# Both feed-forward blocks of a macaron transformer layer in two token halves, routing and combining beside the experts

## Chip, cores and metric

The kernel runs on one core of one Trainium2 chip. The metric is device time in microseconds for one execution: the median of several runs. The kernel before takes 886.95 us (3 runs, 886.47 to 887.26).

## The reference

`x` is 16 sequences of 256 tokens with 256 features, float32; a layer is a half feed-forward block, attention, and the same half feed-forward block again:

```python
x = x + 0.5 * ffn(layernorm(x), gate_w, gate_up_proj, down_proj)
x = x + attn(layernorm(x), w_qkv, w_out)        # 16 heads of 16, causal
x = x + 0.5 * ffn(layernorm(x), gate_w, gate_up_proj, down_proj)

def ffn(x, ...):                                # E = 16 experts, I = 128, TOPK = 2
    p = sigmoid(x @ gate_w.T); p = p / p.sum(-1)
    w, idx = top_k(p, 2); w = w / w.sum(-1)
    combine = sum(one_hot(idx, 16) * w)
    gate, up = split(einsum('th,ehf->etf', x, gate_up_proj))
    y = einsum('eti,eih->eth', silu(gate) * up, down_proj)
    return einsum('eth,te->th', y, combine)
```

The kernel computes only the two experts of each token that `combine` doesn't make zero.

## The kernel before

The 4096 tokens are 32 tiles of 128 (`NT`); `x` stays in SBUF (`x_sb`). Five engines run in-order programs joined by semaphores: PE (matmul), ACT, DVE, POOL and SP, which issues plain DMAs. The order is written by hand: each engine's program is the order of the calls.

A feed-forward block has four stages. In words, with the functions of each engine:

1. Moments and logits. DVE takes moments of `x_sb` (`moments`, 8 token tiles at a time), POOL their inverse root (`inverse_root`, `rstd`), DVE writes the normalised rows (`normalised`, four tiles a round, two buffers `rows`). SP stores them in HBM (`store_normed`, tensor `normed`); a buffer of `rows` is written again only when its store has landed. PE turns the rows (`route_transposes`, L708, four PSUM banks), ACT copies them out (`route_copies`, L846, `xnT`), PE makes logits (L717), ACT copies (L852), PE turns them back (L733), ACT takes the sigmoid (L862).
2. The choice. DVE finds the two best experts of all tokens (L978 to L988), their weights, counts per expert (L997 on, after two PE matmuls), and a slot for each token and choice (L1008 to L1023). Tokens are sorted by expert into tiles of 128 slots. An expert's last tile may be part empty, so there are at most `NE_T` = 4096 x 2 / 128 + 16 = 80 tiles. The expert of each tile is in `eid`.
3. One hots. For each pair of token tile and choice, DVE (L1032, L1033) and ACT (`second_parts`, L880 and L885) make one-hot matrices, and PE adds their product (L750) into a bank, which yields for each slot the token that fills it: `source` (L1043). There are 64 pairs, eight at a time.
4. Tiles. For each of the 80 tiles POOL gathers 128 rows of `normed` by an indirect DMA (`fetch`, L632, a ring of four buffers `xe`), PE turns them (`transpose_in`, L767), ACT copies (`evac_in`, L868, `xeT`), PE multiplies by the expert's weights, which it picks by a register (`gate_up_mm`, L774), ACT takes silu (L872), DVE the product (`gated`, L1049, `hid`), PE turns it (`transpose_hid`, L780), DVE copies (`evac_hid`, L1053, `hidT`), PE multiplies (`down_mm`, L785), DVE copies the result (`evac_out`, L1058, `ye`), SP stores it (`store`, L576, `grouped_out`). PE's order in step j is `transpose_in(j+1)`, `gate_up_mm(j)`, `transpose_hid(j-1)`, `down_mm(j-2)`. PSUM banks, `xeT`, `hid` and `hidT` are double.

Each token's two result rows must come back from `grouped_out`, by indirect DMA on POOL from `slot`, and are added with their weights on DVE. For the first block that is done in attention (`attn_pool` FETCH, L294; `attn_vector` MIX, L497 and L502), two token tiles a sequence. For the last block it follows the tiles: 64 gathers (L649, a ring of eight), two DVE operations a tile (L1081, L1084), and SP stores `out`.

Ahead of attention ACT rearranges the query and key weights (L439) and DVE fills the three `kT` buffers with ones (L488); two of these buffers and the block's work buffers share one memory (`shared`), the third and the raw weights share `spare`. Attention is ordered by tables (`PE_TURN` and others), in which a step is (offset of the sequence, kind, number); they stay as they are.

## Time and profile before

| what | us |
|---|---|
| median of 3 runs | 886.95 |
| the profiled execution, time | 886.32 |
| the profiled execution, span | 884.6 |
| PE busy in the span | 662.1 (75%) |
| DVE busy | 574.8 (65%) |
| ACT busy | 366.6 (41%) |
| POOL busy | 395.4 (45%) |
| first block, first tile turned | 88.06 |
| attention, first rows turned | 242.24 |
| last block, first rows turned | 592.03 |
| last block, first tile turned | 660.34 |
| last block, first gather of results | 798.02 |

Busy shares are means over stages that differ: PE is busy nearly without a gap in the tiles and in attention and idle in the rest. So a stage is to be read by itself, with what each engine waits for in it. PEld is the load of weights into PE, which overlaps the matmuls before; its start shows best when PE takes up a piece of work. The granted clock is the share of 2.4 GHz that PE had: 1.0 is 2.4, 0.5 is 1.2 GHz.

### The profile page before, as it was taken

To read this page: it belongs to the slowest core of one execution; us is meant where nothing else is said; L and a number is where in the kernel's file an instruction comes from. 1 tells how busy PE (TensorE), PEld (TensorE's weight loads), DVE (VectorE), ACT (ScalarE), POOL (GpSimd) and SP (SyncE) were. 2 spreads that over 40 slices of the span, in tenths; PEclk is the share of its full clock that TensorE was granted. 3 is DMA by queue.
4 is the path that set the end of the run, shared out by engine and by line. 5 is a ranking of instruction groups with operands and counts; after the bars stand their busy time and mean duration, and the time that the engine had idled before them with its cause. 6 is when DMAs were issued, how large, how long until landed. Compare 5 with 4: busy or idle time off the path is not lost.

```text
span 884.6 us, 17856 instructions
## 1 busy us (share of the span) xinstructions
PE 662.1 (75%) x5016; PEld 507.6 (57%) x5017; DVE 574.8 (65%) x1599; ACT 366.6 (41%) x941; POOL 395.4 (45%) x467
## 2 busy tenths in 40 slices
PE   2614999999078999999999999866159999990000
PEld 2402888887056777777777777544038888870000
DVE  6597455555758888878888877646964555553333
ACT  2417334444025555555656655454263333430000
POOL 4101655553453554444555422240026555536775
PEclk9955999999678999999999999988559999995555
DMA  7680455557263444444444433014004555574554
GB/s 238 219 258 10 142 162 162 160 160 137 65 185 106 132 128 120 121 116 129 114 109 121 113 107 97 4 48 144 0 24 142 162 162 161 161 130 130 153 152 142
DMA packets 94136, 113.36 MB, mean 128 GB/s; under 512 B 11633, under 2 KB 84609, under 8 KB 94081
## 3 DMA queue, kind: packets, MB, share of 16 engines
q1 hardware_dynamic: 80224, 74.87, 27.5%
q0 software_dynamic: 13824, 37.77, 17.5%
q8 instruction: 31, 0.51, 0.2%
q14 instruction: 25, 0.20, 0.1%
q10 hardware_dynamic: 32, 0.02, 0.0%
HBM read 49.30 MB, written 33.55 MB: 94 GB/s over the span
## 4 chain that ended last, share of the span: by engine, by line
PE 64%; DVE 12%; DMA 8%; issue 5%; POOL 5%; ACT 4%; SPq 1%; DVEq 0%; ACTq 0%; POOLq 0%
PE bank L774 16%; PE bank L785 8%; PE bank L352 6%; PE bank L411 5%; PE bank L372 5%; PE bank L397 5%; PE bank L767 4%; POOL shared L649 4%; DMA shared<-grouped_out,slot 3%; PE bank L359 3%; PE bank L375 3%; PE bank L431 3%; PE bank L780 2%; DMA normed<-shared 2%; ACT shared L885 1%
## 5 line engine op out<-in xcount | busy, mean ns | idle before, releaser
L632 POOL DMA_INDIRECT shared<-normed,source x160 | 152.3, 952 | 213.4 <-DVE source L1043 111.2
L774 PE MATMUL bank<-wgu_sb,xeT 128*128 x640 | 167.8, 386 | 0.0
L306 POOL TENSOR_SCALAR_AFFINE_SELECT pr<-pr 128x512 f32<-128x512 f32 x128 | 81.0, 655 | 154.8 <-ACT pr L476 154.6
L534 DVE TENSOR_REDUCE mx<-bank 128x2 f32<-128x512 f32 (+1 forms) x192 | 127.0, 685 | 23.6 <-PE bank L375 20.4
L1053 DVE COPY hidT<-bank 128x128 f32<-128x128 f32 x160 | 46.6, 291 | 116.8 <-PE bank L780 115.9
L774 PEld LDWEIGHTS bank<-wgu_sb,xeT 128*128 128x128 f32 x640 | 111.5, 194 | 8.8
L476 ACT ACTIVATE pr<-bank 128x512 f32<-128x512 f32 x192 | 102.9, 609 | 30.6 <-PE bank L397 18.1
L785 PE MATMUL bank<-wd_sb,hidT 128*128 x320 | 95.6, 382 | 0.0
L868 ACT COPY xeT<-bank 128x256 f32<-128x256 f32 x160 | 59.5, 372 | 84.6 <-PE bank L767 84.3
L294 POOL DMA_INDIRECT gathered_rows<-grouped_out,slot x64 | 69.0, 1078 | 27.8 <-DMA grouped_out<-shared 13.4
L872 ACT ACTIVATE silu<-bank 128x128 f32<-128x128 f32 x160 | 44.4, 278 | 83.2 <-PE bank L774 83.2
L649 POOL DMA_INDIRECT shared<-grouped_out,slot x64 | 61.3, 958 | 32.4 <-issue 16.1
L767 PE MATMUL bank<-ident,shared 128*128 128x128 f32 x320 | 63.1, 280 | 9.4 <-DMA shared<-normed,source 9.3
L1058 DVE COPY shared<-bank 128x256 f32<-128x256 f32 x160 | 67.9, 424 | 3.5 <-PE bank L785 0.7
L352 PE MATMUL bank<-anT,wqk 128*128 128x256 f32 x256 | 63.4, 394 | 1.9 <-ACT anT L447 1.9
L375 PE MATMUL bank<-future,ident_b 128*128 128x256 bf16 (+1 forms) x192 | 61.3, 319 | 0.0
L767 PEld LDWEIGHTS bank<-ident,shared 128*128 128x128 f32 x320 | 45.1, 144 | 27.5 <-issue 9.3
L411 PE MATMUL bank<-pr,v_sb 128*32 128x256 f32 (+1 forms) x1024 | 54.9, 332 | 3.3 <-POOL pr L306 3.3
L372 PE MATMUL bank<-shared 112*128 112x256 bf16 (+1 forms) x352 | 52.7, 255 | 4.1 <-DMA shared<-parts 3.3
L785 PEld LDWEIGHTS bank<-wd_sb,hidT 128*128 128x128 f32 x320 | 48.3, 191 | 12.4 <-issue 0.4
L1049 DVE TENSOR_TENSOR hid<-bank,silu 128x128 f32<-128x128 f32 x160 | 45.3, 283 | 15.5 <-ACT silu L872 15.5
L352 PEld LDWEIGHTS bank<-anT,wqk 128*128 128x128 f32 x256 | 48.4, 198 | 8.7 <-ACT anT L447 2.8
(148 smaller groups left out, 1118.2 us busy)
## 6 DMA issues: line engine op xcount, KB each, us to landing
grouped_out<-shared SPq DMA_DIRECT2D x160, 128.0 KB, 1.7
shared<-parts SPq DMA_DIRECT2D x154, 128.0 KB
spare<-parts SPq DMA_DIRECT2D x70, 128.0 KB
normed<-shared SPq DMA_DIRECT2D x16, 512.0 KB, 3.1
x_sb<-in_L_attn_x_dram SPq DMA_DIRECT2D x4, 1024.0 KB, 9.7
wgu_sb<-_L_ffn_gate_up_proj_dram SPq DMA_DIRECT2D x8, 512.0 KB, 8.6
out_dram<-x_sb SPq DMA_DIRECT2D x16, 256.0 KB, 2.6
shared<-normed,source POOLq DMA_INDIRECT x160, 2.8
```

The lines of the kernel that those rows point to most:

```text
L306: nc.gpsimd.affine_select(out=m, in_=m, compare_op=ALU.is_ge, fill=0.0, base=0, pattern=[[0, 4], [1, P]], channel_multiplier=-1).then_inc( ...
L352: last = nc.tensor.matmul(dst[:, e * S:(e + 1) * S], wqk[:, c, x, e, :], anT[:, c, :], start=(c == 0), stop=(c == HC - 1))
L372: nc.tensor.matmul(dst[:, i * w:(i + 1) * w], q[0:ROWS, h0 + i, u * P:(u + 1) * P], k[0:ROWS, h0 + i, 0:w], start=(i == 0), stop=False, sk ...
L375: nc.tensor.matmul(diag, ident_b[:, :], future[:, 0:nh, :], start=False, stop=True, skip_group_check=True).then_inc(at["score_done"], 1)
L411: last = nc.tensor.matmul(bankC[j * VW:(j + 1) * VW, cols + kt * P:cols + S], v_sb[b % 2][:, kt, 4 * n + j, :], rhs, start=(kt == 0), stop ...
L476: nc.scalar.activation(dst.rearrange("p h n -> p (h n)"), bank[n % 3][:, :], ACT.Exp).then_inc(at["exp_ready"], 1)
L534: nc.vector.tensor_reduce(mx[:, u, h0:h0 + nh], bank[3 + n % 2][:, :].rearrange("p (h k) -> p h k", h=nh), AX.X, ALU.max).then_inc(at["max ...
L632: nc.gpsimd.indirect_dma_start(xe[:, r, :], None, normed, bass.IndirectOffsetOnAxis(source[:, j:j + 1], 0)).then_inc(s["xe_loaded"][r], 16)
L649: nc.gpsimd.indirect_dma_start(late[:, t % LATE, j, :], None, grouped_out, bass.IndirectOffsetOnAxis(slot[:, t, j:j + 1], 0)).then_inc(s[" ...
L767: last = nc.tensor.transpose(bank[u][:, c * P:(c + 1) * P], xe[:, r, c * P:(c + 1) * P], ident[:, :])
L774: last = nc.tensor.matmul(bank[2 + u][:, 0:2 * I], xeT[:, u, c, :], wgu_sb[:, e, c, :], start=(c == 0), stop=(c == HC - 1))
L785: nc.tensor.matmul(bank[6 + u][:, 0:H], hidT[:, u, :], wd_sb[:, e, :], start=True, stop=True).then_inc(s["down_done"], 1)
```

## The change

Each feed-forward block runs in two halves of 16 token tiles (`HT`), A and B, each with its own `normed`, `grouped`, slots and at most `NH` = 47 tiles; `ES` = 94 tiles a block run in one sequence. The routing of a half is cut into parts (moments, rows, top, counts, one hots and so on), and each engine has a table of (step, part, number). `route` runs a table's parts one after the other: half A, ahead of the tiles. `route_beside` runs those of half B inside the tile loop, after the tile work of the given step. In the last block POOL gathers the results of 13 token tiles of half A in the steps of `GATHER_AT` (53, 56, ... 89), and DVE combines 12 of them in the steps of `COMBINE_AT` (57, 60, ... 90).

Banks are fewer per use: the routing's transposes have bank 5 alone, the tiles' transposes bank 0, `transpose_hid` bank 3 and `down_mm` bank 4. The output copy `evac_out` goes from DVE to ACT. SP loads half A of `x`, then all expert weights, then stores half A's rows, then loads half B of `x` and attention's weights. The fills with ones are written as 32x2048 float32 words: one at the program's start, two at step 49 of the first block. `wqk_in` lies in `gathered_rows`, and the first gather of attention waits for its conversion. Loops with registers are unrolled, the helper `after` is written out, and attention's parts are otherwise the same.

```diff
-def macaron_block(nc, x_in, w_qkv, w_out, gate_w, gate_up, down, out, stages=("ffn", "attn", "ffn")):
...
     EW = 32
-    NE_T = B * S * TOPK // P + E
     RING = 4
-    NK = NE_T // RING
-    LOADS = 4
+    HT = NT // 2
+    NH = (HT * P * TOPK + E * (P - 1)) // P
+    ES = 2 * NH
+    GATHER_AT = range(NH + 6, NH + 45, 3)
+    COMBINE_AT = range(NH + 10, NH + 46, 3)
     LATE = 8
     PLACES = 8
     EPS = 1e-5
...
+    grouped = [nc.dram_tensor(f"grouped{h}", [NH * P, H], F32).ap() for h in range(2)]
 
     ctx = ExitStack()
     with ctx:
...
-        wqk_in = spare[:, 0:HC * 2 * H].rearrange("p (c f) -> p c f", c=HC)
+        wqk_in = gathered_rows[:, 0:2, :, :].rearrange("p r k h -> p (r k h)").rearrange("p (c f) -> p c f", c=HC)
+        ye, xe = (spare[:, i * RING * H:(i + 1) * RING * H].rearrange("p (r h) -> p r h", r=RING) for i in range(2))
...
-            for r in range(RING):
-                dve.wait_ge(ffn[0]["ye_stored"][r], 16 * NK)
-            dve.wait_ge(at["wqk_ready"], 2 * HC)
-            for i in range(BUFS):
-                last = nc.vector.memset(kT[i][ROWS // 32 * 32:P, :, :], 1.0)
-            last.then_inc(at["ones_set"], 1)
...
+        DVE_ROUTE = [(0, STATS, 0), (1, MOMENTS, 0), (2, STATS, 1), (3, NORMALISE, 0), (4, MOMENTS, 1), (5, STATS, 2),
+                     (6, NORMALISE, 1), (7, MOMENTS, 2), (8, STATS, 3), (9, NORMALISE, 2), (10, MOMENTS, 3),
+                     (12, NORMALISE, 3), (19, TOP, 0), (21, TOP, 1), (23, PICKS, 0), (24, WEIGHTS, 0), (26, COUNTS, 0),
...
+        ACT_ROUTE = [(4, TURNED, 0), (7, TURNED, 1), (8, LOGITS, 0), (10, TURNED, 2), (11, LOGITS, 1), (13, TURNED, 3),
+                     (14, LOGITS, 2), (15, LOGITS, 3), (17, SIGMOID, 0), (32, ONEHOT, 0), (35, ONEHOT, 1), (38, ONEHOT, 2),
...
+        PE_ROUTE = [(4, TURNED, 0), (7, TURNED, 1), (7, LOGITS, 0), (10, TURNED, 2), (10, LOGITS, 1), (10, LOGITS_T, 0),
...
+        POOL_ROUTE = [(5, MOMENTS, 0), (8, MOMENTS, 1), (11, MOMENTS, 2), (14, MOMENTS, 3)]
+        SP_ROUTE = [(1, STORE, 0), (4, STORE, 1), (7, STORE, 2), (10, STORE, 3)]
...
+        def route(table, part, g):
+
+            for _, kind, n in table:
+                part(kind, n, g)
+
+        def route_beside(table, part, j, g):
+
+            for at_step, kind, n in table:
+                if at_step == j:
+                    part(kind, n, g)
+
+        def tile_at(f, j):
+
+            return f * ES + j, j // NH, j % NH, 2 * f + j // NH
...
+            def part(kind, n, g):
+                if kind == STORE:
+                    R = g * ROUNDS + n
+                    sp.wait_ge(s["xn_ready"], RING * (R + 1))
+                    sp.dma_start(normed[g % 2].rearrange("(n p) h -> p n h", p=P)[:, n * RING:(n + 1) * RING, :],
+                                 rows[:, R % 2, :, :]).then_inc(s["xn_stored"][R % 2], 16)
+
+            route(SP_ROUTE, part, 2 * f)
...
+                for c in range(HT // RING, NT // RING):
+                    load_x(sp, c)
+                sp.dma_start(wqk_in, w_qkv.rearrange("(c p) f -> p c f", p=P)[:, :, 0:2 * H]).then_inc(wqk_loaded, 16)
+                sp.dma_start(wv[:, :, :], w_qkv.rearrange("(c p) f -> p c f", p=P)[:, :, 2 * H:3 * H]).then_inc(wv_loaded, 16)
+                sp.dma_start(wout_sb[:, :, :], w_out.rearrange("(c p) f -> p c f", p=P)).then_inc(wout_loaded, 16)
+            for j in range(ES):
+                G, p, jj, g = tile_at(f, j)
+                route_beside(SP_ROUTE, part, j, 2 * f + 1)
+                sp.wait_ge(s["ye_ready"], G + 1)
+                sp.dma_start(grouped[p][jj * P:(jj + 1) * P, :], ye[:, G % RING, :]).then_inc(s["ye_stored"][G % RING], 16)
...
+            for c in range(HT // RING):
+                load_x(sp, c)
+            for e in range(0, E, 4):
+                for c in range(HC):
+                    sp.dma_start(wgu_sb[:, e:e + 4, c, :],
+                                 gate_up[e:e + 4, c * P:(c + 1) * P, :].rearrange("e p f -> p e f")).then_inc(wgu_loaded, 16)
+                sp.dma_start(wd_sb[:, e:e + 4, :], down[e:e + 4].rearrange("e i h -> i e h")).then_inc(wd_loaded, 16)
...
+            def gather(t):
+                if t == 0:
+                    stored_through(pool, ES + NH)
+                if t == HT:
+                    stored_through(pool, 2 * ES)
+                if t - LATE + 1 > 0:
                     pool.wait_ge(s["x_done"], t - LATE + 1)
                 for j in range(TOPK):
-                    nc.gpsimd.indirect_dma_start(late[:, t % LATE, j, :], None, grouped_out,
+                    nc.gpsimd.indirect_dma_start(late[:, t % LATE, j, :], None, grouped[t // HT],
                                                  bass.IndirectOffsetOnAxis(slot[:, t, j:j + 1], 0)).then_inc(s["gathered"][t % LATE], 16)
+
+            route(POOL_ROUTE, part, 2 * f)
+            for j in range(ES):
+                G, p, jj, g = tile_at(f, j)
+                if jj == 0:
+                    pool.wait_ge(s["source_ready"], g + 1)
+                    for i in range(2):
+                        pool.wait_ge(s["xn_stored"][i], 16 * (ROUNDS // 2) * (g + 1))
+                if G - RING + 1 > 0:
+                    pool.wait_ge(s["xe_transposed"], G - RING + 1)
+                nc.gpsimd.indirect_dma_start(xe[:, G % RING, :], None, normed[p],
+                                             bass.IndirectOffsetOnAxis(source[:, p, jj:jj + 1], 0)).then_inc(s["xe_loaded"][G % RING], 16)
+                route_beside(POOL_ROUTE, part, j, 2 * f + 1)
+                if f == 1 and j in GATHER_AT:
+                    gather(GATHER_AT.index(j))
+            if f == 1:
+                for t in range(len(GATHER_AT), NT):
+                    gather(t)
...
+            def part(kind, n, g):
+                R = g * ROUNDS + n
+                if kind == TURNED:
+                    for r in range(RING):
+                        pe.wait_ge(s["xn_ready"], R * RING + r + 1)
+                        if R * RING + r > 0:
+                            pe.wait_ge(s["xnT_ready"], R * RING + r)
+                        for c in range(HC):
+                            last = nc.tensor.transpose(bank[5][:, c * P:(c + 1) * P], rows[:, R % 2, r, c * P:(c + 1) * P], ident[:, :])
+                        last.then_inc(s["xn_transposed"], 1)
...
+                elif kind == ONEHOT:
+                    for r in range(PLACES):
+                        i = n * PLACES + r
+                        pe.wait_ge(s["onehot_ready"], g * HT * TOPK + i + 1)
+                        if r % TOPK:
+                            pe.wait_ge(s["second_ready"], g * HT + i // TOPK + 1)
+                        nc.tensor.matmul(bank[7][:, 0:NH], is_part[:, r, :], is_tile[:, r, 0:NH], start=(i == 0),
+                                         stop=(i == HT * TOPK - 1), skip_group_check=True).then_inc(s["source_done"], 1)
...
+            def transpose_in(j):
+                G, p, jj, g = tile_at(f, j)
+                pe.wait_ge(s["xe_loaded"][G % RING], 16 * (G // RING + 1))
+                if G > 0:
+                    pe.wait_ge(s["xeT_ready"], G)
...
+                    last = nc.tensor.transpose(bank[0][:, c * P:(c + 1) * P], xe[:, G % RING, c * P:(c + 1) * P], ident[:, :])
+                last.then_inc(s["xe_transposed"], 1)
...
+            transpose_in(0)
+            read_expert(0)
+            for j in range(ES + 2):
+                if j + 1 < ES:
+                    transpose_in(j + 1)
+                if j < ES:
+                    gate_up_mm(j)
+                if j + 1 < ES:
+                    read_expert(j + 1)
+                if 0 <= j - 1 < ES:
+                    transpose_hid(j - 1)
+                if 0 <= j - 2 < ES:
+                    down_mm(j - 2)
+                route_beside(PE_ROUTE, part, j, 2 * f + 1)
...
+            def part(kind, n, g):
+                R = g * ROUNDS + n
+                if kind == TURNED:
+                    for r in range(RING):
+                        act.wait_ge(s["xn_transposed"], R * RING + r + 1)
+                        if R - 1 > 0:
+                            act.wait_ge(s["logitsT_done"], R - 1)
+                        nc.scalar.copy(xnT[:, R % 2, r, :, :].rearrange("p c n -> p (c n)"), bank[5][:, 0:H]).then_inc(s["xnT_ready"], 1)
...
+                elif kind == SIGMOID:
+                    act.wait_ge(s["logits_done"], ROUNDS * (g + 1))
+                    if g > 0:
+                        act.wait_ge(s["picks_ready"], g)
+                    nc.scalar.activation(prob[:, :, :], bank[7][:, :].rearrange("p (t w) -> p t w", w=EW)[:, :, 0:E], ACT.Sigmoid)\
+                        .then_inc(s["prob_ready"], 1)
...
+                    act.sem_inc(act_turn, 1)
+                    for q in range(m):
+                        nc.scalar.activation(distance[:, q, :], lane_h[:, :], ACT.Abs, bias=minus_part[:, n * m + q:n * m + q + 1])\
+                            .then_inc(s["distance_ready"], 1)
+                    for q in range(m):
+                        act.wait_ge(s["distance_ready"], i + q + 1)
+                        if i * TOPK + q * TOPK + 2 - PLACES > 0:
+                            act.wait_ge(s["source_done"], i * TOPK + q * TOPK + 2 - PLACES)
+                        nc.scalar.activation(is_part[:, q * TOPK + 1, :], distance[:, q, :], ACT.Relu, scale=-1.0, bias=one_e[:, 0:1])\
+                            .then_inc(s["second_ready"], 1)
...
+            def evac_out(j):
+                G, p, jj, g = tile_at(f, j)
+                act.wait_ge(s["down_done"], G + 1)
+                if 16 * (G // RING) > 0:
+                    act.wait_ge(s["ye_stored"][G % RING], 16 * (G // RING))
+                nc.scalar.copy(ye[:, G % RING, :], bank[4][:, 0:H]).then_inc(s["ye_ready"], 1)
...
+            evac_in(0)
+            for j in range(ES + 2):
+                if j + 1 < ES:
+                    evac_in(j + 1)
+                if j < ES:
+                    silu_gate(j)
+                if 0 <= j - 2 < ES:
+                    evac_out(j - 2)
+                route_beside(ACT_ROUTE, part, j, 2 * f + 1)
...
+            route(DVE_ROUTE, part, 2 * f)
+            for j in range(ES + 1):
+                if 0 <= j - 1 < ES:
+                    evac_hid(j - 1)
+                if j < ES:
+                    gated(j)
+                route_beside(DVE_ROUTE, part, j, 2 * f + 1)
+                if f == 0 and j == NH + 2:
+                    for i in range(2):
+                        dve.wait_ge(s["xn_stored"][i], 16 * ROUNDS)
+                        nc.vector.memset(kT_words[i], TWO_ONES).then_inc(at["ones_set"], 1)
+                if f == 1 and j in COMBINE_AT:
+                    combine(COMBINE_AT.index(j))
+            if f == 1:
+                for t in range(len(COMBINE_AT), NT):
+                    combine(t)
...
```

Three places in the engines' programs, word for word (line numbers are those of each kernel).

SP at the start of the program; `x_sb` is the input, `wgu_sb` and `wd_sb` the expert weights, `normed` the stored rows. Before:

```order
L600 DMA x_sb<-in_L_attn_x_dram 128x8x256 x4
L578 UNCONDITIONAL_BRANCH
L578 ISA
L571 ISA
L571 DMA normed<-shared 128x4x256
```

And in the change:

```order
L613 DMA x_sb<-in_L_attn_x_dram 128x4x256 x4
L621 DMA wgu_sb<-in_L_ffn_gate_up_proj_dram 128x4x256 x2
L623 DMA wd_sb<-in_L_ffn_down_proj_dram 128x4x256
L621 DMA wgu_sb<-in_L_ffn_gate_up_proj_dram 128x4x256 x2
L623 DMA wd_sb<-in_L_ffn_down_proj_dram 128x4x256
L621 DMA wgu_sb<-in_L_ffn_gate_up_proj_dram 128x4x256 x2
L623 DMA wd_sb<-in_L_ffn_down_proj_dram 128x4x256
L621 DMA wgu_sb<-in_L_ffn_gate_up_proj_dram 128x4x256 x2
L623 DMA wd_sb<-in_L_ffn_down_proj_dram 128x4x256
L595 DMA normed<-shared 128x4x256 x4
```

The twelve weight loads, which stood behind all stores of rows, now stand ahead of the first.

ACT beside the tiles of half A, steps 16 to 18 (`shared<-bank` of L861 is the sigmoid of half B, `spare<-bank` the output copy). Before there was only the pair of copy and silu for each tile:

```order
L868 COPY xeT<-bank 128x256
L872 ACTIVATE silu<-bank 128x128
L867 REGISTER_ALU
L868 COPY xeT<-bank 128x256
L872 ACTIVATE silu<-bank 128x128
```

In the change:

```order
L884 COPY xeT<-bank 128x256
L889 ACTIVATE silu<-bank 128x128
L896 COPY spare<-bank 128x256
L861 ACT_TABLE_LOAD
L861 ACTIVATE shared<-bank 128x256
L884 COPY xeT<-bank 128x256
L889 ACT_TABLE_LOAD
L889 ACTIVATE silu<-bank 128x128
L896 COPY spare<-bank 128x256
```

The output copy has joined, and a sigmoid with two loads of the function table stands between two tiles.

POOL in the last block; `spare<-normed` or `shared<-normed` is the fetch of a tile, `<-grouped` a gather of results. Before:

```order
L621 TENSOR_TENSOR rstd<-var,minus_half 128x8 x4
L632 DMA shared<-normed,source 128x256 x80
L649 DMA shared<-grouped_out,slot 128x256 x64
```

In the change, from the fetches behind the last root to the end (the pair of rows that repeats is shown twice):

```order
L667 DMA spare<-normed,source 128x256 x39
L655 DMA shared<-grouped,slot 128x256 x2
L667 DMA spare<-normed,source 128x256 x3
L655 DMA shared<-grouped,slot 128x256 x2
L667 DMA spare<-normed,source 128x256 x3
```

```order
L655 DMA shared<-grouped,slot 128x256 x2
L667 DMA spare<-normed,source 128x256 x4
L655 DMA shared<-grouped,slot 128x256 x38
```

26 of the 64 gathers have moved in between the fetches, two for every three fetches.

## Rows read from the trace of the kernel before

**Rows 1.** Stretches: each engine's busy us (x instructions), then clock, DMA share, GB/s

```profile
634.00:657.00 23.00, 11.81 (x64) 6.25 (x64) 20.66 (x101) 20.84 (x65) 0.00 (x0) 0.50 0.01 1
661.00:795.00 134.00, 133.31 (x718) 111.29 (x718) 70.53 (x240) 51.98 (x160) 73.57 (x77) 0.98 0.56 153
```

**Rows 2.** Timeline of one tile: start, us, engine line operation xcount [idle before]

```profile
151.62 0.36 PEld L767 LDWEIGHTS bank<-ident,shared 128*128 128x128 f32 x2
...
152.26 0.37 ACT L868 COPY xeT<-bank 128x256 f32<-128x256 f32 x1 [0.48 <-PE bank L767]
...
152.71 0.14 PEld L780 LDWEIGHTS bank<-ident,hid 128*128 128x128 f32 x1
...
153.23 0.29 DVE L1053 COPY hidT<-bank 128x128 f32<-128x128 f32 x1 [0.77 <-PE bank L780]
153.25 0.36 PEld L767 LDWEIGHTS bank<-ident,shared 128*128 128x128 f32 x2
153.44 0.28 DVE L1049 TENSOR_TENSOR hid<-bank,silu 128x128 f32<-128x128 f32 x1
```

**Rows 3.** Timeline, last block: the last output matmuls, the first and last gather

```profile
793.61 1.21 PE L785 MATMUL bank<-wd_sb,hidT 128*128 x4
...
798.02 0.95 POOL L649 DMA_INDIRECT shared<-grouped_out,slot  x1 [13.20 <-DMA grouped_out<-shared]
...
877.58 0.96 POOL L649 DMA_INDIRECT shared<-grouped_out,slot  x1 [0.30 <-issue]
```

**Rows 4.** Timeline, last block: start of the choice, first fetch, first transpose

```profile
613.83 0.69 DVE L978 TENSOR_REDUCE top<-shared 128x32 f32<-128x512 f32 x1 [3.72 <-ACT shared L862]
...
657.31 1.02 POOL L632 DMA_INDIRECT shared<-normed,source  x1 [55.59 <-DVE source L1043]
...
660.34 0.66 PE L767 MATMUL bank<-ident,shared 128*128 128x128 f32 x2 [4.13 <-DMA shared<-normed,source]
```

**Rows 5.** Timeline, first block: the first tile is turned

```profile
88.06 0.66 PE L767 MATMUL bank<-ident,shared 128*128 128x128 f32 x2 [4.30 <-DMA shared<-normed,source]
```

**Rows 6.** Timeline between the first block's tiles and attention

```profile
220.22 2.24 ACT L439 ACTIVATE wqk<-spare 128x256 f32<-128x256 f32 x4
...
220.99 1.20 PE L785 MATMUL bank<-wd_sb,hidT 128*128 x4
...
229.98 3.47 DVE L488 MEMSET shared<- 32x4096 bf16 x1 [0.80 <-issue]
...
237.75 0.88 DVE L497 SCALAR_TENSOR_TENSOR mix<-gathered_rows,weight,x_sb 128x256 f32<-128x256 f32 x2
...
242.24 1.08 PE L342 MATMUL bank<-ident,an 128*128 128x128 f32 x4 [20.04 <-DVE an L519]
```

**Rows 7.** Timeline, last block's routing: rows turned and copied at two clocks

```profile
592.03 3.28 PEld L708 LDWEIGHTS bank<-ident,shared 128*128 128x128 f32 x16 [4.50 <-DVE shared L934]
...
592.76 3.36 ACT L846 COPY shared<-bank 128x256 f32<-128x256 f32 x8 [4.95 <-PE bank L708]
...
601.36 1.17 PEld L708 LDWEIGHTS bank<-ident,shared 128*128 128x128 f32 x8 [0.66 <-DVE shared L934]
...
601.84 1.34 ACT L846 COPY shared<-bank 128x256 f32<-128x256 f32 x4 [0.88 <-PE bank L708]
```

**Rows 8.** Tile `x_sb`: ns min/median/max, first and last start; then landing times

```profile
L600 SPq DMA_DIRECT2D x_sb<-in_L_attn_x_dram x4: 447/1338/2832, 0.8 to 4.1; - x4
...
DMA to landing us min/median/max: 6.0/9.7/11.6
```

**Rows 9.** Timeline, last block's routing: a root, logits, and rows that wait

```profile
595.24 1.76 POOL L621 TENSOR_TENSOR rstd<-var,minus_half 128x8 f32<-128x8 f32 x1 [1.93 <-DVE var L931]
...
598.28 0.65 PE L717 MATMUL bank<-shared,gwT 128*32 128x128 f32 x16
...
605.68 1.38 DVE L934 TENSOR_SCALAR shared<-x_sb,mean,rstd 128x256 f32<-128x256 f32 x4 [1.94 <-DMA normed<-shared]
```

**Rows 10.** Timeline, first block: ACT loads its function table

```profile
83.36 1.28 ACT L893 ACT_TABLE_LOAD   x1
```

847 lines of the change are left out of this document (358 added, 489 removed).

## The prediction, made before the changed kernel was run

> **What bounds the kernel now.** I read the stages first [rows 1]: in the last block's tile stage PE is busy for 133 of 134 us at a clock of 0.98, while ACT, DVE and POOL have time left. One tile then shows the order in which they need each other [rows 2]: its first weight load is at 151.62, the next tile's at 153.25, so a tile costs **1.63 us** and PE sets it. The 80 tiles of the last block take from 660.34 to 794.82 = 134.5 us [rows 3, 4]. Ahead of that stands the routing: moments and logits to 613.8, a chain of DVE operations on 128x512 to 634, one hots up to the first indirect fetch at 657.31, which takes 3.0 us to the transpose [rows 4]. PE idles or waits in most of it. Behind it stand 64 gathers that POOL issues one per 1.263 us ((877.58 - 798.02)/63) until the span ends at 884.6 [rows 3]. The first block has its first tile at 88.06 [rows 5] and a hole of 20.05 us of PE, 222.19 to 242.24, before attention [rows 6]. So the places to win are real: routing, hole and tail. But what hides them must be laid beside a PE with nothing to spare.
>
> **More tiles.** A half needs (16x128x2 + 16x127)/128 = 47 tiles, so a block does 94 for 80. 14 x 1.63 = 22.8, both blocks **+45.6**. Nothing hides it: PE sets the pace. Certain to some 2 us.
>
> **The routing of half A** comes alone before the tiles. In the last block: four rounds of moments, root and rows, but PE turns each of 16 token tiles through one bank and waits for ACT's copy of the one before. One such turn is the start of the load to the start of the copy (0.73 at 592.03, low clock; 0.48 at 601.36, high clock), the copy 0.37 [rows 2], and I allow 0.05 for the way back: 1.15 or 0.90 [rows 7]. 16 x 1.15 = 18.4 and 3.9 for logits and their tail, 22.3; all 32 tiles take 21.8 now (592.03 to 613.83). The DVE chain has half the elements: 0.69 becomes 0.42 (between 0.28 for 128x128 and 0.69 for 128x512), 20.3 becomes 13.5. Of the 23.1 of one hots ACT's 64 operations are 20.9 (20.84 busy [rows 1]), so half A needs 10.4 + 2.2; the fetch 3.0 as now. 51.4, less 0.6 of shorter first moments, against 68.3 from 592.03 to 660.34: **-17.5**. At the high clock throughout 4 more; bounds -17 and -22.
> In the first block SP issues 12 weight loads (6.3 MB) right behind 2.1 MB of x. The four x loads now, 4.2 MB issued in 6 us, land up to 11.6 us after their issue [rows 8], the last near 15.7: some 280 GB/s, and they queue. So the 8.4 MB are in near 30 us; the first rows stored come behind them, and rows of round 2 wait for that store, as they do now at 605.68 [rows 9]. Round 2 at 31, turns of rounds 2 and 3 to 41, tail 3.5, chain 13.5, one hots 12.6, fetch 3.0: first tile near 73.6, **-14.5**. If stores are not held up, 63: -25.
> The Trainium skill (DMA: Bandwidth & Descriptors, "Queues, rings and completion order") says that each DMA engine consumes one ring's descriptors in order, though a later one may finish its write earlier; the landing times agree. By it the stores wait; without it this term is -25 and the sum 946.
>
> **Routing of half B beside A's tiles.** Engines are in order, so a lump delays the next tile's work once it is longer than the gap. Gaps from one tile [rows 2]: DVE has `hid` done 0.47 into a tile's period and must have served the next `hidT` and `hid` by 1.08 of the one after: a lump of up to 1.7 is free. ACT now also copies the outputs: 0.37 behind a down_mm that is 0.6 long [rows 3] and follows the load at 1.08, so from 0.4 to 0.8 of the next period. Its copy of `xeT`, then done at 1.2, must be there at 1.63: a lump of L costs L - 0.45. PE has no gap: all it does or waits for counts. Per half, in order:
> - the root on POOL (between 0.72 and 1.76, about 1.05 [rows 9]) waits for DVE's moments ahead of fetch 6: 0.7.
> - 4 times TURNED: PE sits in it while PE and ACT alternate, three turns of 0.90, the last load 0.2 and 0.35 for ACT's output copy: 3.25, x 4 = 13.0. NORMALISE (1.38 for four [rows 9]) is inside DVE's gap.
> - logits: 4 x 0.6 [rows 9], four turns 0.1 each, and 1.1 once where PE waits for ACT's copy of round 2: 3.8.
> - SIGMOID: two table loads of 1.28 [rows 10] with a sigmoid and a copy of 0.37 between them: 2.1.
> - DVE lumps: TOP 2.7 and 2.25, COUNTS 2.7, SLOT 2.7, over 1.7 by 1.0 + 0.6 + 1.0 + 1.0, and 0.5 of PE: 4.1.
> - ONEHOT 4 times: ACT's eight at 0.326 (20.84 busy for 64 [rows 1]) = 2.6, costs 2.1; PE then waits for DVE's twelve (2.3) to 3.0 of a period of 1.62: 1.4. 3.5 x 4 = 14.1.
> - source numbers come at step 45, the fetch takes 3.3 more, tile 47 is wanted at 46: 2.5.
> Sum 40.3, both blocks **+80.6**. Lower bound: PE's own instructions alone, 32 turns x 0.11, logits 2.4, turns, counts and ids 0.9, 32 placings x 0.1 = 9.9, so 20 in both. Upper bound: the same with PE at 1.2 GHz for a while, below. I take the sum, since each lump is in the queue of an engine that a tile needs.
> Of table loads the Trainium skill (ScalarE: Activation LUTs, "What ACT_TABLE_LOAD costs") says 1.28 us for the load and 1.38 more for a drain. In this trace the row shows 1.28 and starts right behind the operation before it. By the page the sum would be 5.5 higher.
>
> **Hole before attention.** The three memsets leave it: two go into half B's tiles. 32x2048 float32 has no row: by elements it is half of the 3.47 of 32x4096 bf16, by bytes the same, and each may bring its 0.8 gap [rows 6]. Two by elements, one gap hidden, are 4.0, less the free 1.7: **+2.3**; bounds 0 and +6.8. But `wqk_in` now lies in `gathered_rows`, so the gathers wait for ACT's four wqk conversions behind its last output copy: 0.45 + 2.24 after PE's end. First gather at +2.8, the fourth landed at +9.6 (three more at 1.26 and 3.0); from MIX to PE it is 4.5 now (237.75 to 242.24), and the root stands behind eight gathers, 0.4 more: +14.5 against 20.05, **-5.5**. Late next is the gather, not DVE. Between 0 and -16.
>
> **Tail.** In half B of the last block 13 token tiles are gathered between fetches, and 12 combined. For three tiles POOL has 3 fetches and 2 gathers, 6.3 us, for PE's 4.9: POOL becomes the pace. Count from tile 50's transpose: fetch 53 at 0.6, then 66 issues x 1.26, the last fetch goes out at 83.8. Its tile needs 3.0, three periods of 4.9 and a store and start of 3.2 (794.82 to 798.02), so half B's rows can be gathered from 94.9 (six gathers of half A fit in between); 32 x 1.26 = 40.3, and 7.0 from the last issue's start to the end less its 1.26: 141.0. Without hiding it would be 73.5 (PE's tiles) + 89.8 (794.82 to 884.6) = 163.3. **-22.3**; all 26 hidden free would be -33.
>
> **Sum.** 884.6 + 45.6 + 80.6 + 2.3 - 14.5 - 17.5 - 5.5 - 22.3 = 953.3. The profiled execution took 886.32 for its span of 884.6 (+1.7), and the median of the runs is 0.6 above it: **956 us**, 7.7% slower. Attention's order and PE's instructions there are the same and I count 0.
>
> **Rivals.**
> A. Half of the lumps is absorbed (ACT and DVE catch up more than I allow, the four fetched tiles buffer): beside-cost 25 a half, 925. For it: DVE is busy for 53% and ACT for 39% of the stage [rows 1]. Against: averages; the chain of one tile has only the gaps above.
> B. The clock falls. In the one hots PE is half busy and the granted clock is 0.50, in the tiles 0.98 [rows 1]. Beside TURNED and ONEHOT PE waits again and again. At 1.2 GHz a PE-paced tile is twice 1.63; for a dozen tiles a half +19, 994.
> C. The cover holds: beside-cost 9.9 a half, 892.5 + 2.3 = 895, still 0.9% slower.
> D. Faster. As C, and stores are not queued behind the weights (-10) and A's turns run at the high clock (-4): 881. It decides from a beside-cost of 13 us a half downward, with both early starts.
> E. Only the stores are free: 946.
>
> **How the numbers follow.** The sum as worked out, 940 to 972: 0.49. E 0.07, A 0.19, B 0.12, C 0.06, D 0.06, rest 0.01. The range 900 to 990 leaves out C and D and the upper half of B. Under 0.2% (1.8 us) a measurement can't tell from no change. Faster 0.06, same 0.01, slower 0.93.
>
> **What would show it.** A tile period of 1.63 in half B of the first block and 94 transposes a block; the first tile near 73 and, in the last block, 54 after its first moments; A's 47 tiles taking near 117 us where B's take 77; PE waiting for ACT's `xnT` copy between turns; a wait for `normed` of 10 us or more on DVE near 17 to 31; the first gather behind L439; POOL with no idle from fetch 53 on. The forecast is wrong if A's 47 tiles take under 95 us or over 140, if the clock in them is under 0.9, or if POOL waits for PE in the last half.

## The result, and the profile after

The changed kernel takes **959.1 us** (median of 4 runs, 954.2 to 963.0) beside 887.1 for the kernel before on the same chip: ratio 1.081, interval 1.075 to 1.086. The prediction was 956. The profiled execution took 954.18 for a span of 952.4 at a mean clock of 0.93; 953.3 was forecast for the span. It is the fastest of the four: the median is 3.1 above the forecast. What follows compares spans.

The stages of the changed kernel, in the columns of [rows 1] (a stretch, busy us of PE, PEld, DVE, ACT and POOL with instructions, granted clock, DMA share, GB/s). In order: routing of half A, A's tiles, B's tiles, the hole, attention, and in the last block half A's routing, A's tiles, B's tiles with the combine, the tail.

```profile
0.00:71.00 71.00, 21.36 (x137) 10.59 (x137) 36.58 (x145) 19.75 (x55) 12.32 (x34) 1.00 0.60 195
71.00:185.00 114.00, 94.43 (x547) 71.66 (x548) 54.95 (x231) 61.36 (x192) 49.50 (x52) 0.99 0.42 124
185.00:270.00 85.00, 81.67 (x435) 67.61 (x435) 27.40 (x99) 44.70 (x144) 42.14 (x45) 0.98 0.55 146
270.00:284.00 14.00, 0.17 (x1) 0.00 (x0) 3.16 (x11) 2.46 (x5) 8.72 (x10) 0.60 0.31 92
284.00:632.00 348.00, 326.61 (x3040) 241.95 (x3040) 269.05 (x620) 190.36 (x402) 154.04 (x200) 0.99 0.39 108
632.00:683.00 51.00, 20.29 (x135) 10.09 (x135) 28.75 (x119) 18.47 (x54) 5.13 (x6) 0.56 0.13 44
683.00:800.00 117.00, 97.12 (x549) 73.58 (x550) 50.47 (x215) 61.37 (x193) 50.53 (x52) 0.94 0.40 121
800.00:902.00 102.00, 83.62 (x433) 64.65 (x431) 35.87 (x125) 46.33 (x144) 73.10 (x77) 1.00 0.60 163
902.00:952.00 50.00, 0.38 (x2) 0.00 (x0) 17.60 (x37) 0.37 (x1) 30.66 (x32) 0.52 0.56 173
```

The second and the seventh row are the beside-stages: PE is busy for 83% there and not for 99 as in [rows 1], and PE is the engine that sets the pace of a tile. B's tiles in the first block (third row) are again nearly all PE. In B's tiles of the last block POOL has 77 operations and PE is at 82%.

| stretch | before | after | forecast | measured |
|---|---|---|---|---|
| start to the first tile | 88.06 | 71.02 | -14.5 | -17.0 |
| first block's tiles | 134.1 | 199.2 | +65.4 | +65.0 |
| hole before attention | 20.05 | 14.4 | -5.5 | -5.7 |
| attention | 349.8 | 348.1 | 0 | -1.7 |
| last block, first turn to first tile | 68.3 | 50.7 | -17.5 | -17.6 |
| last block, first tile to the end | 224.3 | 269.1 | +40.8 | +44.8 |
| sum | 884.6 | 952.4 | +68.7 | +67.8 |

**Start.** Timeline of the changed kernel (start, us, engine, line and operation, in brackets the idle time before it and who ended it): DVE's rows of round 2, the first fetch, the first turn of a tile.

```profile
29.18 1.38 DVE L958 TENSOR_SCALAR shared<-x_sb,mv,rstd 128x256 f32<-128x256 f32 x4 [14.40 <-DMA normed<-shared]
...
68.02 1.16 POOL L667 DMA_INDIRECT spare<-normed,source  x1 [35.88 <-DVE source L1027]
...
71.02 0.29 PEld L772 LDWEIGHTS bank<-ident,spare 128*128 128x128 f32 x2 [3.67 <-issue]
```

DVE stood 14.4 us for the store of round 0's rows, as in [rows 9], where it was 1.94. The first tile is at 71.02, where [rows 5] has 88.06.

**A's tiles.** The copies of `xeT`, one a tile, give the period: in B's tiles of the first block it is 1.62 or 1.63 in 42 of 46 cases. In A's tiles it is not. One lump of four turns, then one lump of one hots, both in the first block:

```profile
80.81 0.36 PEld L732 LDWEIGHTS bank<-ident,shared 128*128 128x128 f32 x2
...
81.49 0.38 ACT L851 COPY shared<-bank 128x256 f32<-128x256 f32 x1
...
81.98 0.20 PEld L732 LDWEIGHTS bank<-ident,shared 128*128 128x128 f32 x2 [0.82 <-issue]
...
83.90 0.20 PEld L732 LDWEIGHTS bank<-ident,shared 128*128 128x128 f32 x2 [0.76 <-issue]
...
84.38 0.37 ACT L851 COPY shared<-bank 128x256 f32<-128x256 f32 x1 [0.59 <-PE bank L732]
...
84.65 0.38 ACT L884 COPY xeT<-bank 128x256 f32<-128x256 f32 x1
```

```profile
158.49 1.28 ACT L872 ACTIVATE shared<-lane_h,minus_part 128x128 f16<-128x128 f16 x4
...
159.66 1.26 ACT L878 ACTIVATE shared<-shared,one_e 128x128 f16<-128x128 f16 x4
160.83 0.35 ACT L884 COPY xeT<-bank 128x256 f32<-128x256 f32 x1
...
161.30 0.20 PEld L772 LDWEIGHTS bank<-ident,spare 128*128 128x128 f32 x2 [1.90 <-issue]
```

In the first, PE's turns go out at 80.81 and then one per 0.96, each after ACT's copy; ACT copies the tile's `xeT` only at 84.65, 4.79 after the one before. In the second, ACT's eight operations sit ahead of `xeT` and PE waits 1.90. The sigmoid between two tiles, with its two table loads:

```profile
119.65 1.28 ACT L861 ACT_TABLE_LOAD   x1
120.94 0.38 ACT L861 ACTIVATE shared<-bank 128x256 f32<-128x256 f32 x1
...
121.61 1.28 ACT L889 ACT_TABLE_LOAD   x1
122.90 0.28 ACT L889 ACTIVATE silu<-bank 128x128 f32<-128x128 f32 x1
```

All the excess over 1.63, by stretches of tiles:

| beside A's tiles | forecast | first block | last block |
|---|---|---|---|
| root, turns, logits (tiles 5 to 18) | 17.5 | 16.8 | 18.4 |
| sigmoid (18 to 22) | 2.1 | 2.1 | 2.1 |
| choice on DVE (22 to 33) | 4.1 | 2.7 | 2.7 |
| one hots (33 to 46) | 14.1 | 13.8 | 13.9 |
| fetch for tile 47 | 2.5 | 1.8 | 1.7 |
| the first five tiles | 0 | 0.0 | 0.7 |
| sum | 40.3 | 37.1 | 39.5 |

**The two fills** beside half B (the fills of [rows 6], as float32 words; the second starts at 194.34), and the transposes of `hid` that waited:

```profile
192.20 1.76 DVE L1059 MEMSET shared<- 32x2048 f32 x1 [0.48 <-issue]
...
196.68 0.14 PEld L798 LDWEIGHTS bank<-ident,hid 128*128 128x128 f32 x1 [2.75 <-DVE hid L1038]
...
199.06 0.23 PEld L798 LDWEIGHTS bank<-ident,hid 128*128 128x128 f32 x1
```

A fill takes 1.76. Both together hold PE for 2.75, and the tile behind runs with weight loads of 0.23 where 0.14 is usual, a low clock, which costs 1.6 more: 4.4 in all for 2.3 forecast. The 1.6 doesn't come every time: in the profile of experiment 7 the same two fills cost 2.8 and the tile behind them takes 1.63.

**The hole.** The last output matmul, ACT's conversion, the first gather, the second mix, PE's first transposes of attention; in [rows 6] the gather did not wait for ACT, and the mix waited for DVE's fills:

```profile
269.48 0.69 PE L806 MATMUL bank<-wd_sb,hidT 128*128 x2 [0.66 <-ACT spare L896]
...
270.48 2.19 ACT L427 ACTIVATE wqk<-gathered_rows 128x256 f32<-128x256 f32 x4
272.94 0.94 POOL L271 DMA_INDIRECT gathered_rows<-grouped,slot  x1 [13.57 <-ACT wqk L427]
...
279.51 0.48 DVE L483 SCALAR_TENSOR_TENSOR mix<-gathered_rows,weight,x_sb 128x256 f32<-128x256 f32 x1 [2.10 <-DMA gathered_rows<-grouped,slot]
...
284.53 1.09 PE L322 MATMUL bank<-ident,an 128*128 128x128 f32 x4 [14.36 <-DVE an L506]
```

**The last half.** POOL, last block: the first gather of half A beside half B's tiles, the last fetch, the last gather that needs no result of B, the first that does. Then the waits of that stage (us in all, times, longest).

```profile
808.07 0.96 POOL L655 DMA_INDIRECT shared<-grouped,slot  x1 [2.87 <-DMA grouped<-spare]
...
890.31 0.96 POOL L667 DMA_INDIRECT spare<-normed,source  x1 [0.30 <-issue]
...
897.88 0.96 POOL L655 DMA_INDIRECT shared<-grouped,slot  x1 [0.30 <-issue]
905.34 0.95 POOL L655 DMA_INDIRECT shared<-grouped,slot  x1 [6.50 <-DMA grouped<-spare]
```

```profile
PEld bank L772 <- DMA spare<-normed,source: 24.5, 18, 3.1
...
POOL shared L655 <- DMA grouped<-spare: 2.9, 1, 2.9
POOL spare L667 <- PE bank L772: 1.5, 5, 0.3
```

Between 808 and 898 POOL is never idle for more than 0.31, in line with the forecast. The 1.5 us for PE are five gaps of 0.3, as long as the 0.30 that stand before its other issues, so PE never held it up. PE waits 24.5 for fetched rows. The first gather holds POOL for 2.87, since A's last results are still being stored, and the last fetch leaves 15.0 us before B's results are in.

### The profile page after: what moved, and what is told of

The parts are those of the page before. It is cut to its first block, busy times and chain, and to the rows that moved or that the text cites. A ratio compares the mean times of both kernels' runs of the same rounds, so it can differ in the third digit from the quotient of the medians.

```text
span 952.4 us, 17170 instructions
## 1 busy us (share of the span) xinstructions
PE 725.6 (76%) x5274; PEld 540.1 (57%) x5274; DVE 523.8 (55%) x1599; ACT 445.2 (47%) x1189; POOL 426.2 (45%) x503
## 3 DMA queue, kind: packets, MB, share of 16 engines
q0 software_dynamic: 15168, 41.44, 17.6%
## 4 chain that ended last, share of the span: by engine, by line
PE 59%; DVE 11%; POOL 9%; DMA 6%; ACT 6%; issue 6%; SPq 2%; POOLq 0%; ACTq 0%; DVEq 0%
PE bank L789 11%; PE bank L806 6%; PE bank L399 5%; PE bank L333 5%; PE bank L355 5%; PE bank L383 5%; POOL shared L655 4%; PE bank L772 3%; POOL spare L667 3%; DMA spare<-normed,source 3%; PE bank L358 3%; PE bank L340 3%; PE bank L419 3%; PE bank L732 2%; PE bank L798 2%
## 5 line engine op out<-in xcount | busy, mean ns | idle before, releaser
L667 POOL DMA_INDIRECT spare<-normed,source x188 | 180.7, 961 | 237.8 <-PE bank L772 140.4
L789 PE MATMUL bank<-wgu_sb,xeT 128*128 x752 | 200.8, 391 | 0.0
L806 PE MATMUL bank<-wd_sb,hidT 128*128 x376 | 116.3, 391 | 1.7 <-ACT spare L896 1.3
L772 PE MATMUL bank<-ident,spare 128*128 128x128 f32 x376 | 76.4, 286 | 43.1 <-DMA spare<-normed,source 28.6
L896 ACT COPY spare<-bank 128x256 f32<-128x256 f32 x188 | 69.9, 372 | 61.3 <-PE bank L806 61.3
L772 PEld LDWEIGHTS bank<-ident,spare 128*128 128x128 f32 x376 | 49.8, 145 | 70.7 <-DMA spare<-normed,source 34.4
L271 POOL DMA_INDIRECT gathered_rows<-grouped,slot x64 | 69.6, 1088 | 26.2 <-ACT wqk L427 13.6
L655 POOL DMA_INDIRECT shared<-grouped,slot x64 | 61.3, 957 | 28.3 <-issue 18.0
L732 PE MATMUL bank<-ident,shared 128*128 128x128 f32 x128 | 33.5, 354 | 47.0 <-ACT shared L851 26.4
L798 PE MATMUL bank<-ident,hid 128*128 128x128 f32 x188 | 52.7, 281 | 6.7 <-DVE hid L1038 6.6
```

The source lines that it names most:

```text
L655: nc.gpsimd.indirect_dma_start(late[:, t % LATE, j, :], None, grouped[t // HT], bass.IndirectOffsetOnAxis(slot[:, t, j:j + 1], 0)).then_in ...
L667: nc.gpsimd.indirect_dma_start(xe[:, G % RING, :], None, normed[p], bass.IndirectOffsetOnAxis(source[:, p, jj:jj + 1], 0)).then_inc(s["xe_ ...
L772: last = nc.tensor.transpose(bank[0][:, c * P:(c + 1) * P], xe[:, G % RING, c * P:(c + 1) * P], ident[:, :])
L789: last = nc.tensor.matmul(bank[1 + G % 2][:, 0:2 * I], xeT[:, G % 2, c, :], wgu_sb[:, e, c, :], start=(c == 0), stop=(c == HC - 1))
L798: nc.tensor.transpose(bank[3][:, 0:P], hid[:, G % 2, :], ident[:, :]).then_inc(s["hid_transposed"], 1)
L806: nc.tensor.matmul(bank[4][:, 0:H], hidT[:, G % 2, :], wd_sb[:, e, :], start=True, stop=True).then_inc(s["down_done"], 1)
```

## Experiments

The chips differ, so each kernel is given by its ratio to the kernel before on its own chip. The control, the changed kernel run again, was at 1.0863 [1.083, 1.0896].

**1. Turns in single token tiles** (`turns_spread`), **2. one hots in single token tiles** (`onehots_spread`), **3. both** (`both_spread`). Only the steps beside tiles change (in short, not the lines of the code):

```diff
-  (4, TURNED, 0), (7, TURNED, 1), ...      # four turns each
+  for each: a turn at a, a, a + 1, a + 2; logits two steps later
-  (33, ONEHOT, 0), (36, ONEHOT, 1), ...    # four token tiles each (DVE; ACT from 32, PE from 34)
+  for each: one token tile at a, a, a + 1, a + 2 (the last group: a, a, a + 1, a + 1)
```

> The half-B routing beside A's tiles has its 16 turns (PE transpose, ACT copy) cut from four lumps of four into single turns, two at one step and one at each of the next two; logits and what follows two steps later. Theory (a lump costs what exceeds the gap of its engine): the tiles from 5 to 18 of the first block take 16.8 us more than 13 periods of 1.63, of it some 13 for the lumps; a single copy of 0.37 fits ACT's 0.45, two at one step exceed it by 0.3, PE's own part stays: 3 to 4 us are left of 16.8. So 13 less a half, both blocks 26: 928 of 954. Rival (each added operation costs its own time, however it is cut): ACT's 16 copies are 5.9 and PE's turns 1.8, all of it stays, no change within 3 us. Second rival (PE waits lower its clock and most of the cost is that): the gain is over 30 and the runs lie closer together.

> The one hots of half B are cut from four lumps of four token tiles into single token tiles, two at one step and one at the next two. Theory of lumps and gaps: tiles 33 to 46 now take 13.8 us over 13 periods of 1.63. ACT needs 2.6 us for three steps, its gaps in three steps are 3 x 0.45 to 3 x 0.6, so 0.8 to 1.3 is left per group, 4 to 5 a half; PE no longer waits for eight places at a time. 9 less a half, 18 in both: 936 of 954. Rival (work costs its time however cut): ACT's 10.4 a half stay, at most 3 us a half gained, 948 or more.

> Both cuts together: the sums add, 26 + 18 = 44, so 910 of 954; still some 23 above the kernel before, because 28 more tiles at 1.63 (45.6) stay. Rival (work costs its time): 948 or more. If turns and one hots share one cause (clock), the two gains overlap and the result is over 918.

Measured: 1.0839 [1.0794, 1.0884], 1.0886 [1.0832, 1.094] and 1.0726 [1.0698, 1.0754]. By the sums 26, 18 and 44 us were to go. The kernel before took 896 us on this chip, and half B of the last block ran otherwise there (below), so A's tiles decide. With the turns cut, tiles 5 to 18 of the first block have 12.9 in excess where they had 16.8, and in the last block 12.0 for 18.4: **4 and 6 saved and not 13**. The 16.8 is the lowest that the profiles of kernels with whole lumps show in this stretch (16.8 to 21.7 in the first block, 18.3 or 18.4 in the last). The one hots have 7.3 for 13.8: 6.5 saved, 9 expected. Half A of the first block, first to last tile, is 100.6 with both for 110.2. Why the turns gave so little is in `turns_spread`, a step with two turns and one with a single turn (PE's weight loads; L746 turns, L786 is the next tile's transpose):

```profile
96.20 0.36 PEld L746 LDWEIGHTS bank<-ident,shared 128*128 128x128 f32 x2
...
97.38 0.20 PEld L746 LDWEIGHTS bank<-ident,shared 128*128 128x128 f32 x2 [0.82 <-issue]
...
97.54 0.25 PEld L786 LDWEIGHTS bank<-ident,spare 128*128 128x128 f32 x2
...
99.25 0.36 PEld L746 LDWEIGHTS bank<-ident,shared 128*128 128x128 f32 x2
...
99.58 0.25 PEld L786 LDWEIGHTS bank<-ident,spare 128*128 128x128 f32 x2
```

A single turn keeps PE for 99.58 - 99.25 = **0.33**, and that step took 1.92 for 1.63: ACT's copy is hidden, PE's own part is not. The prediction's lower bound had 0.11 for each of the two 128x128 transposes of a turn, so 0.22. Two turns at one step still wait 0.82 for ACT between them. 16 turns of 0.33, four waits of 0.82 and the prediction's 4.5 for root and logits are 13.1, an estimate that fits the 12.9. So both theories were wrong in part: PE's own work stays, as the rival said, and what goes is part of the waits for the round trip between PE and ACT.

**4. Weights behind the row stores** (`weights_behind`).

```diff
-  x loads of half A; 12 weight loads; row stores of half A
+  x loads of half A; row stores of half A; 12 weight loads
```

> SP issues the 12 expert weight loads (6.3 MB) behind the four row stores of half A and not ahead of them. Theory (stores queue behind the loads): DVE's wait of 14.4 us before the rows of round 2, until 29.18, becomes under 3, round 2 is turned right behind round 1, and the first tile stands 9 to 12 us earlier than 71.0, near 60; the weights are in by some 47, so nothing else waits: 943 of 954. Rival 1 (the wait is something else, for example the x loads): no change. Rival 2 (the weights then come too late): first tile later than 63, gain under 7.

```profile
17.94 1.38 DVE L958 TENSOR_SCALAR shared<-x_sb,mv,rstd 128x256 f32<-128x256 f32 x4 [1.77 <-PE bank L732]
...
60.09 0.29 PEld L772 LDWEIGHTS bank<-ident,spare 128*128 128x128 f32 x2 [3.75 <-issue]
```

DVE's wait of 14.4 is gone (its rows of round 2 now wait 1.77, for PE) and the first tile is at 60.09: 10.9 earlier, as the first theory had it. The time was 1.0862 [1.0819, 1.0905] all the same, where 943 of 954 was expected: A's tiles of the first block took 115.7 for 110.2, at a clock of 0.83 to 0.91 from 60 to 120 us (experiment 9 is about that), and half B of the last block took 121.2, as slow as in all four kernels on this chip.

**5. The control** (`after_again`) and **6. no routing of half B** (`no_route_b`).

> The changed kernel itself, as the control on the chip of this job. In the two kernels of the first job whose last half is the same code, half B of the last block took 119 to 122 us from its first to its last tile, where the changed kernel's profile has 97, with waits of ACT and PE that have no releaser; the kernel before took 896 there and 887 on the other chip. If that is the chip's, a control on that chip shows half B at 115 or more and a ratio near 1.088; on a chip like the first it shows 97 and 1.081.

Half B of the last block took 96.4, first to last tile, on this third chip, as in the first profile (97.0). The 119 to 122 were seen in all four kernels on the chip of experiments 1 to 4 and in none elsewhere; the changed kernel itself did not run on that chip. The ratio is 1.0863 all the same, where 1.081 was expected with a half B of 97. In the profile A's tiles of the first block make up most of the difference: 114.8 for 110.2, with the clock at 0.88 in the stretch of the turns (experiment 9).

```diff
-  for at_step, kind, n in table: if at_step == j: part(kind, n, g)
+  pass
...                         # half B's tiles read source, experts and slots of half A
```

> Leaves out the whole routing of half B (moments, rows, turns, logits, choice, one hots): its tiles take half A's rows, experts and slots. 94 tiles, the combine beside them and all else stay. Theory: all that A's tiles take over 47 x 1.63 is this routing, 37.1 us in the first block and 39.3 in the last, so 76 us go and A's tiles run at 1.63 throughout: ratio to the kernel before 0.99 to 1.00. Rival (the tiles of two halves are slower for another reason: fetches, clock): under 60 us go, ratio over 1.01.

The kernel leaves out half B's routing, so its output is not that of the layer. Measured: **0.9926** [0.9907, 0.9945], 879.1 us; 82 less than the control (960.9). A's 47 tiles ran at 1.63 (75.2 and 74.6, first to last). Laid beside the tiles, the routing costs more than the whole change loses; and with none of it the change wins 0.7%. The 1.63 also shows that single PSUM banks and the output copy on ACT cost a tile nothing.

**7. No gathers beside half B** (`tail_alone`).

```diff
-  GATHER_AT = range(NH + 6, NH + 45, 3);  COMBINE_AT = range(NH + 10, NH + 46, 3)
+  GATHER_AT = COMBINE_AT = range(0)
```

> No gather and no combine beside half B's tiles of the last block: all 32 token tiles are gathered behind them. Forecast: hiding 13 of them is worth 22.3 us; the ledger of the profile makes it some 17.5, since the first gather holds POOL for 2.9 us while A's last tile is stored, and the fetches land late among the gathers. So slower than the changed kernel by 17 to 18 (half B of the last block at 77 us, the tail at 89). Rival (gathers and fetches on one POOL cost as much as they hide): within 5 us of the control. On a chip where half B takes 120 us the rival should win.

```profile
872.95 0.96 POOL L655 DMA_INDIRECT shared<-grouped,slot  x1 [0.30 <-issue]
...
884.25 0.69 PE L806 MATMUL bank<-wd_sb,hidT 128*128 x2 [0.65 <-ACT spare L896]
```

Measured 1.0904 [1.0884, 1.0924], 0.4% above the control, whose interval it touches. In the profiles the last block, from its first tile on, is 4.2 longer (273.1 for 268.9), and not 17: the rival's figure, on a chip where half B took 96. The rows (first gather, last output matmul) show why. Since half A's results lie in a tensor of their own, POOL starts on them 11 us before PE's last matmul, without being told to; in the kernel before the first gather waits until 798.02, 3.2 behind it [rows 3]. The last gather goes out at 952.57. From tile 47 on, POOL has 47 fetches and 64 gathers at 1.26 in either order. To lay gathers beside fetches saves only the time in which POOL would wait for PE, and part of that was given back here as fetches that land late.

**8. The fills as float32 words, alone** (`before_fill`, made from the kernel before).

```diff
-  nc.vector.memset(kT[i][ROWS // 32 * 32:P, :, :], 1.0)                      # bf16
+  nc.vector.memset(words[ROWS // 32 * 32:P, :], 1.0 + 127.0 / 2 ** 16)       # the same bits, float32
```

> The kernel before with one thing of the change: the three fills of kT ahead of attention write the same bits as float32 words (32x2048) in place of bf16 (32x4096); nothing is moved. A fill of words takes 1.76 in the changed kernel's profile and 3.47 as bf16 [rows 6], so the chain of three ends at 232.6 in place of 237.7, where the fourth gather has just landed: the hole before attention shrinks by 5.1 us to 15, ratio 0.994. Rival (the gathers set the end of the hole anyway): under 2 us.

```profile
224.67 1.76 DVE L489 MEMSET shared<- 32x2048 f32 x1 [2.63 <-DMA grouped_out<-shared]
...
226.81 1.76 DVE L489 MEMSET shared<- 32x2048 f32 x1 [0.38 <-issue]
...
236.40 1.08 PE L342 MATMUL bank<-ident,an 128*128 128x128 f32 x4 [14.82 <-DVE an L520]
```

The third fill starts at 228.95. Measured: **0.9942** [0.9924, 0.996], 880.2 us, as expected. The hole of [rows 6] is 14.8 for 20.05. This one line, taken out of the change, beats both kernels.

**9. PE kept at work in its waits** (`warm_turns`).

```diff
   last.then_inc(s["xn_transposed"], 1)
+  if g % 2 and r < RING - 1:                  # beside tiles, two matmuls nobody reads
+      ...                                   # once, a wait until bank 7 is free
+      for _ in range(2):
+          nc.tensor.matmul(bank[7][:, 3 * P:4 * P], ident, wgu_sb[:, 0, 0, 0:P], start=True, stop=True)
```

> Beside A's tiles PE does two 128x128 matmuls of no use behind each of the first three turns of a lump, in the 0.82 us in which it waits for ACT's copy. Two such matmuls are 0.3 us of PE, so they delay nothing. Theory (what makes the runs of the changed kernel spread over 7 to 9 us is PE's clock, which falls to 0.83 to 0.91 in some stretches with turns: there the tile behind a lump takes 2.5 to 2.7 for 1.83): the clock stays at 0.97 or more from 80 to 120 us, the gaps behind the lumps are 5.5 and 1.83 throughout, 2 to 6 us faster than the changed kernel. Rival (the fall has another cause, or PE's waits in a lump are not what lowers it): no change, the same 6.2 and 2.7 in some lumps.

The same two stretches of the control, then of `warm_turns` (columns as above, the clock stands ahead of the DMA share):

```profile
78.00:122.00 44.00, 36.42 (x226) 27.24 (x225) 16.34 (x71) 19.45 (x62) 19.36 (x20) 0.88 0.42 133
122.00:185.00 63.00, 53.19 (x284) 40.46 (x283) 34.84 (x143) 37.66 (x119) 24.13 (x26) 0.97 0.39 114
```

```profile
78.00:122.00 44.00, 41.78 (x298) 34.02 (x297) 18.15 (x79) 22.19 (x69) 21.40 (x22) 1.00 0.48 145
122.00:185.00 63.00, 52.26 (x280) 39.13 (x279) 34.91 (x144) 37.30 (x119) 23.88 (x26) 1.00 0.39 110
```

The clock is 1.00 for 0.88 in the stretch of turns. One pair of profiles can't show the cause: in the first profile of the changed kernel this stretch had 1.00 as well. What does is tiles 5 to 18 over all profiles. Five kernels with whole lumps of turns (the changed kernel, the control, experiments 2, 4 and 7) give ten such stretches: one has 16.8 in excess, nine 18.3 to 21.7. `warm_turns` has 16.8 and 16.7. Behind the third lump two tiles take 5.57 and 1.84, where the control has 6.46 and 2.51. A's tiles take 110.8 and 110.3 in the two blocks, for 114.8 and 112.8. The time is **1.0741** [1.0713, 1.0769], 0.6% below the first measurement of the changed kernel, whose interval it touches, and 1.1% below the control, each on a chip of its own. So work of no use took away the excess of the low clock in these tiles; how much the whole kernel gains is less certain. The runs spread over 5 us, for 7 to 9.

**10. Both halves routed ahead of the tiles** (`routed_ahead`), on each engine and its queue:

```diff
   route(PE_ROUTE, part, 2 * f)
+  route(PE_ROUTE, part, 2 * f + 1)            # and nothing of it beside the tiles
```

> Half B is routed right behind half A and ahead of the tiles; nothing is laid beside the tiles but the combine. Theory: beside, it costs 37 to 39 a half; alone it costs what half A's does in the last block, from the first turn to the last one hot, some 46 to 48 (turns and logits 23, choice 13.5, one hots 11), and A's tiles then run at 1.63. So about 9 slower in each block than the changed kernel, ratio 1.10 to 1.11: laying it beside saves a fifth of it, no more. Rival (beside is no better than alone, since PE stands either way): within 4 us of the changed kernel's 1.081 to 1.088.

Measured 1.0983 [1.0962, 1.1004], just under the 1.10 to 1.11 that were expected and outside the rival's range. It is 1.2% over the control, 10.6 us for both blocks; its first tile stands 48 us later (119.9 for 72.0 at the first copy of `xeT`) and its A tiles are at 1.63. So 48 us alone were some 37 to 42 beside. By the ratios the overlap is worth 10.6 for both blocks against the control and 15.4 against the first measurement, by the profiles' spans 15 and 22: 5 to 11 a block.

**11. All together** (`split_best`): experiments 3 and 4, and

```diff
-  if j == NH + 2: two fills of 32x2048
+  if NH + 2 <= j < NH + 10: one fill of 32x512 at each step
-  GATHER_AT = range(NH + 6, NH + 45, 3);  COMBINE_AT = range(NH + 10, NH + 46, 3)
+  GATHER_AT = range(NH + 8, NH + 47, 3);  COMBINE_AT = range(NH + 12, NH + 48, 3)
```

> What the runs so far point to, together: turns and one hots of half B in single token tiles (9.5 us in the first block's profile, 12.5 in the last, against the control), weights behind A's row stores (10 at the start), the two fills beside tiles in eight pieces of 0.44 (4.4), the gathers beside half B two steps later, so that the first no longer waits 2.9 for A's last store. Sum 22 + 10 + 4.4 + 2.9 = 39, some 922 where the control has 961 and the kernel before 886: ratio 1.04. It can't reach the kernel before, since with no routing of half B at all the ratio is 0.993 and 27 us a block of it are left. Rival (PE's waits only move to other places): ratio over 1.06.

Measured **1.0319** [1.0299, 1.0338], 917.3 us for 922 expected. The parts were not timed one by one. Half B of the first block takes 75.7 with the fills in pieces (79.4 before), the first gather no longer waits, and behind half B's first fetch POOL's only wait above 0.31 is the one for B's results:

```profile
869.41 0.95 POOL L679 DMA_INDIRECT shared<-grouped,slot  x1 [5.24 <-DMA grouped<-spare]
```

It is the best version of the split, and 3% slower than the kernel before.

## Why the prediction was right, and where it was not

- **More tiles, +45.6**: right, the period is 1.63 where nothing is laid beside (42 of 46 in B's tiles of the first block, and A's 47 in `no_route_b`).
- **Routing beside, +80.6**: measured 76.6, and `no_route_b` takes away 82 against its control. Each stretch came within 1.4. The parts inside a turn were less sure than the sum: PE's own share is 0.33 a turn where the lower bound took 0.22 (32 transposes of 0.11), which lifts that bound of 9.9 a half (its terms add to 10.0) by 1.8. And cutting the lumps gave 4 to 6 where the model of gaps gave 13. Turns and one hots cut small leave 27 a half (`both_spread`), `split_best` 28. Rivals C and D needed 9.9 and 13 or less; no arrangement that was run came near.
- **Rival A** (half the lumps absorbed): excluded, 37 and 39 where it needed 25.
- **Rival B** (the clock falls): the mechanism is there, its size is not. It was no dozen tiles at 1.2 GHz but the tiles behind a lump, in some executions. It costs up to 5 a half (21.7 for 16.8 in tiles 5 to 18). That it makes the runs of the changed kernel spread over 7 to 9 us is likely, not shown: those of the kernel before spread over 1 on the first chip but over 4 to 6 on two others. In the profile it is small (0.99 in A's tiles of the first block, 0.94 in the last).
- **Table loads**: the stretch with the sigmoid cost 2.1, as the row of 1.28 gives it. The sigmoid and the silu each start right at the end of their load, 1.29 behind its start. With the drain of 1.38 a load that the Trainium skill names (ScalarE: Activation LUTs, "What ACT_TABLE_LOAD costs") it would have been 4.9, an estimate (2.1 and two drains); this trace does not bear that out.
- **The start, -14.5**: -17.0. The mechanism (stores behind the weights) was right and experiment 4 shows it; the first tile at 63 of rival E would have been 60. The size was 2.5 off: the store was in by 29.2, for 31, and from there to the first fetch it took 38.8, for 39.6.
- **Last block's routing, -17.5**: -17.6. **Hole, -5.5**: -5.7, and the gather is what came last, as named (the mix waits 2.10 for it).
- **The fills, +2.3**: +4.4. The two fills hold PE for 2.75, and the clock falls behind them in this profile.
- **The tail, -22.3**: this step failed. From tile 50's transpose to the end it took 148.2 for 141.0: 2.3 until the last fetch (the wait of 2.87 for A's last store, less 0.6 of an earlier start), 3.9 between it and B's first gather (tile 93 was turned 6.1 after its fetch went out among the gathers, 3.0 were allowed) and 1.0 in the last 32 gathers. The baseline was wrong too. By the prediction's own rows 94 tiles take 134.5 + 22.8 from the first to PE's end; less 50 periods of 1.63 that is 75.8, and with the 89.8 behind it 165.6, not 163.3. So the gain is 165.6 - 148.2 = 17.4 for 22.3. And most of it is not from gathers beside tiles, which are worth 4 (`tail_alone`), but from the split of the tensor of results, to which the prediction gave no price: it lets the gathers start ahead of PE's end. The remaining 13 follow from these rows; no run has the split tensor by itself.
- **Attention, 0**: -1.7, with the same 3040 matmuls and a clock of 0.99 for 0.97 in the stage. The profiles of the eleven experiments have 347.2 to 350.1 there, so the 1.7 is scatter.

The sum was 0.9 off, since +4.9 in the tail and +2.1 in the fills stood against -4.0 beside the tiles, -2.5 at the start and -1.7 in attention. That it came so close is luck; that every stage moved as forecast, and that the routing beside the tiles is what loses, is not.

## What to carry to other kernels

Before work is laid beside a stage, price it on the engine that paces that stage by how long one of its operations keeps that engine, weight loads included, and then add each round trip to another engine; cutting lumps smaller removed only part of the round trips here. Where one engine issues everything (111 issues of 1.26 us here), another order of issues can win no more than that engine's idle time (4 us here, for 22 forecast). Take a change apart and time the part that costs nothing alone: here a fill written in wider words was worth more than the restructuring around it.

## What the runs showed of the hardware that was not expected

- With useless matmuls in PE's waits the granted clock was 1.00 over 44 us of turns, where the control had 0.88, and A's tiles took 4.0 and 2.5 us less than in the control. The first profile of the changed kernel had 1.00 there without them; over ten stretches that is the exception (experiment 9).
- A fill went with its elements and not its bytes: 32x2048 float32 took 1.76, 32x4096 bf16 3.47. The prediction had taken elements, with bytes as its bound.
- On the chip of experiments 1 to 4 the kernel before took 896 us where it took 886 to 888 on the others, and half B of the last block 119 to 122 for 96 to 98. There ACT and PE stand for up to 3.2 us with no releaser shown, as here in `both_spread`:

```profile
834.58 0.28 ACT L919 ACTIVATE silu<-bank 128x128 f32<-128x128 f32 x1 [3.19 <-issue]
...
835.86 0.18 PEld L824 LDWEIGHTS bank<-ident,hid 128*128 128x128 f32 x1 [3.16 <-issue]
```

  Some records of PE are missing in these stretches. Whether it is the loading of instructions, the DMA traffic or something else of that chip stays open; no run told them apart.
